# Block 1's rotary halves on VectorE, weight loads spread one per unit, weight rounding moved between units, and a separate load for the pooling columns

## The reference

```python
x = x + attn(cond(x))                                # cond: tanh scores, masked softmax, pooled
h = einsum("bsd,bdh->bsh", x, W[cat_ids]) + b[cat_ids]
tidx, tw = gate(h)                                   # 64 experts in 8 groups, 4 groups kept, top 8
y = sum over e of w_dense[:, e] * (silu(h @ wg[e]) * (h @ wu[e])) @ wd[e]
x = x + y + (silu(h @ ws_g) * (h @ ws_u)) @ ws_d     # one shared expert
```

## Time and profile before

| what | value |
|---|---|
| median of 3 runs | 741.04 us (739.32 to 742.67) |
| the profiled execution | 741.32 us |
| span of its trace | 739.5 us |
| TensorE busy | 709.9 us, 96% of the span |
| VectorE busy | 547.2 us, 74% |
| ScalarE busy | 444.7 us, 60% |
| GpSimd busy | 425.2 us, 57% |
| mean granted TensorE clock | 0.989 of full speed |

### The profile page before, as it was taken

How to read it: one execution, slowest core, us unless ns; L and a number is a source line. 1 busy time by engine, 2 the same in 40 slices (tenths; PEclk the granted TensorE clock), 3 DMA queues, 4 the chain that set the end, 5 groups by cost and what they waited for, 6 DMA issues and landing times.

```text
span 739.5 us, 15765 instructions
## 1 busy us (share of the span) xinstructions
PE 709.9 (96%) x5628; PEld 547.5 (74%) x5628; DVE 547.2 (74%) x1144; ACT 444.7 (60%) x857; POOL 425.2 (57%) x352
## 2 busy tenths in 40 slices
PE   8878899999999999999999999999999999999997
PEld 7756676677877778777787777777787777877885
DVE  5766659886598676887688865987768876886664
ACT  3865766568455765568555684557654685555553
POOL 2644488665466644556455654666455564666665
PEclk9998999999999999999999999999999999999999
DMA  8453542445433434434454463434535345444451
GB/s 279 143 199 90 148 108 82 130 106 157 103 123 111 140 110 116 143 96 143 109 120 132 108 154 104 121 108 137 119 115 140 100 142 117 101 123 147 129 134 44
DMA packets 66750, 93.00 MB, mean 126 GB/s; under 512 B 7760, under 2 KB 26640, under 8 KB 66672
## 3 DMA queue, kind: packets, MB, share of 16 engines
q1 hardware_dynamic: 62784, 88.07, 43.4%
q10 hardware_dynamic: 3888, 3.93, 1.5%
HBM read 88.37 MB, written 3.15 MB: 124 GB/s over the span
## 4 chain that ended last, share of the span: by engine, by line
PE 72%; DVE 11%; ACT 9%; issue 3%; POOL 2%; DMA 2%; SPq 1%; POOLq 0%; ACTq 0%; DVEq 0%
PE banks L979 70%; DVE act_w L946 3%; DVE hid L958 2%; ACT s_t L402 2%; ACT hid_hi L535 2%; POOL hid_lo L633 2%; ACT banks L523 1%; ACT L523 1%; ACT L402 1%; PE banks L1059 1%; SPq L269 1%; DMA k_rope<-rope_sum 1%; DVE head_max L704 1%; DVE s_t L703 1%; ACT v_blk L389 1%
## 5 line engine op out<-in xcount | busy, mean ns | idle before, releaser
L633 POOL TENSOR_TENSOR hid_lo<-hid,hid_hi 128x512 fp32r<-128x512 f32 (+1 forms) x264 | 341.9, 1295 | 275.4 <-ACT hid_hi L535 270.3
L946 DVE TENSOR_TENSOR act_w<-banks,cwb 128x512 f32<-128x512 f32 x254 | 174.6, 687 | 126.6 <-ACT banks L523 123.5
L523 ACT ACTIVATE banks<-banks 128x512 f32<-128x512 f32 x254 | 147.2, 582 | 141.3 <-PE banks L979 138.9
L535 ACT CAST hid_hi<-hid 128x512 fp32r<-128x512 f32 (+1 forms) x264 | 162.7, 616 | 76.8 <-DVE hid L958 75.1
L958 DVE TENSOR_TENSOR hid<-act_w,banks 128x512 f32<-128x512 f32 (+1 forms) x264 | 181.3, 687 | 24.8 <-PE banks L979 2.7
L979 PE MATMUL banks<-c_hi,wg_hi 128*128 128x512 f32 x264 | 119.2, 452 | 4.2 <-DVE act_w L946 4.2
L979 PE MATMUL banks<-hid_hi,wd_hi 128*128 128x512 f32 (+1 forms) x264 | 107.1, 406 | 4.7 <-POOL hid_lo L633 4.4
L979 PE MATMUL banks<-hid_hi,wd_lo 128*128 128x512 f32 (+1 forms) x264 | 104.0, 394 | 0.0
L979 PE MATMUL banks<-hid_lo,wd_hi 128*128 128x512 f32 (+1 forms) x264 | 104.0, 394 | 0.0
L979 PE MATMUL banks<-c_lo,wg_hi 128*128 128x512 f32 x264 | 103.9, 394 | 0.0
L979 PE MATMUL banks<-c_hi,wg_lo 128*128 128x512 f32 x264 | 103.9, 394 | 0.0
(11 more groups left out here) (158 smaller groups left out, 805.7 us busy)
## 6 DMA issues: line engine op xcount, KB each, us to landing
cwb<-cw_scratch SPq DMA_DIRECT2D x254, 256.0 KB, 3.7
k_blk<-in_cond_w SPq DMA_DIRECT2D x112, 64.0 KB
xf<-in_x_feat SPq DMA_DIRECT2D x8, 256.0 KB, 4.1
out_feat<-y ACTq DMA_DIRECT2D x8, 256.0 KB, 3.4
wg_raw<-in_we_gate SPq DMA_DIRECT2D x7, 256.0 KB, 5.5
wu_raw<-in_we_up SPq DMA_DIRECT2D x7, 256.0 KB, 5.8
wd_raw<-in_we_down SPq DMA_DIRECT2D x7, 256.0 KB, 5.9
xf<-in_x_tok SPq DMA_DIRECT2D x6, 256.0 KB, 2.8
```

What stands on the lines that cost most here:

```text
L523: nc.scalar.activation(dst, gate_bank(p)[:, :], ACT.Silu).then_inc(S["silu_done"], 1)
L535: nc.scalar.copy(hid_hi[0:n, p % NH, :], hid[0:n, p % NH, :]).then_inc(S["hi_ready"], 1)
L633: nc.gpsimd.tensor_sub(hid_lo[0:n, p % NH, :], hid[0:n, p % NH, :], hid_hi[0:n, p % NH, :].bitcast(F32)).then_inc(S["lo_ready"], 1)
L946: nc.vector.tensor_mul(act_w[:, p % NH, :], gate, weight)\
```

## The change

It has five parts. (1) Block 1's two rotary halves are added by VectorE (they were added by GpSimd) right after c_lo of block 0, and the key half is moved to k_rope by a VectorE copy (it was a DMA on SP's queue). Step 5 of block 1 on TensorE waits for the copy. (2) SP's quarter tiles 14 to 23 are no longer issued in one go: the units 2 to 11 of block 0 issue one each, behind the unit's cwb load, and unit 12 issues the shared expert's. (3) A table SPLITS says which unit of block 0 rounds which quarter tile: 4 takes 10; 6 to 16 take 11 to 21; 26, 27 and 28 take 22, 23 and 24. (4) The first 34 columns of w (w1, b1, vcol, which were at its end) come in a DMA of their own, first of all; the rest of w comes after the first x block with a semaphore of its own (proj_in), and the fold moves behind scores(0) on TensorE. On ScalarE pool_exp(0) moves ahead of the copies of the folded weights. (5) The seven x blocks are issued by ScalarE at its start, x tokens of block 1 by ScalarE too, block 0's residual load moves behind the condition matrices on SP, the blank matmuls go from 14 to 8, and pool_scores(2) moves from behind step 17 to behind step 16 of block 0 on TensorE.

```diff
@@ SP
-            sp.dma_start(c[:, :], consts).then_inc(S["consts_in"], 16)
-            sp.dma_start(w[:, :], weights).then_inc(S["consts_in"], 16)
+            cond = W_COLS["kvT"][0]
+            sp.dma_start(w[:, 0:cond], weights[:, 0:cond]).then_inc(S["cond_in"], 16)
+            sp.dma_start(c[:, :], consts).then_inc(S["consts_in"], 16)
+            sp.dma_start(pt_i, prompt).then_inc(S["prompt_in"], 16)
             sp.dma_start(xf_in[0], x_feat[:, bass.ts(0, TOK)]).then_inc(S["x_in0"], 16)
-            sp.dma_start(pt_i, prompt).then_inc(S["prompt_in"], 16)
+            sp.dma_start(w[:, cond:], weights[:, cond:]).then_inc(S["proj_in"], 16)
...
-            sp.wait_ge(S["c2tok_ps"], 1)
-            for i in range(14, NSPLIT):
-                weight_load(i)
-            sp.dma_start(wg_raw[:, NPAIR, :], ws_gu).then_inc(S["ws_in"], 16)
-            sp.dma_start(wd_raw[0:F, NPAIR, :], ws_down).then_inc(S["ws_in"], 16)
-            attention_loads("keys", 1)
...
+                if not prev and 2 <= p < 12:
+                    if p == 2:
+                        sp.wait_ge(S["c2tok_ps"], 1)
+                    weight_load(p + 12)
@@ ScalarE
-            act.wait_ge(S["consts_in"], 32)
+            for i in range(1, NBLK):
+                act.dma_start(xf_in[i], x_feat[:, bass.ts(i, TOK)]).then_inc(S["x_in1" if i < 4 else "x_in2"], 16)
+            act.wait_ge(S["cond_in"], 16)
+            act.wait_ge(S["consts_in"], 16)
             pool_hidden(0)
+            pool_exp(0)
+            act.wait_ge(S["proj_in"], 16)
@@ ScalarE and GpSimd, in the unit
+        SPLITS = {4: 10, **{p: p + 5 for p in range(6, 17)}, 26: 22, 27: 23, 28: 24}
-                if not prev and BEFORE_UNITS <= p + 1 <= NSPLIT:
-                    split(p + 1)
+                if not prev and p in SPLITS:
+                    split(SPLITS[p])
@@ GpSimd
-            rope_add(1)
@@ VectorE, after rotate(1) and rest_of_input(0, 0)
+                    dve.wait_ge(S["rot_ready"], 2)
+                    dve.wait_ge(S["rope_score_ps"], 1)
+                    nc.vector.tensor_add(rope_sum[:, :], rot[:, 0, :], rot[:, 1, :]).then_inc(S["rope_summed"], 1)
+                    keys_moved(1)
@@ TensorE
-        WARM_BLANK = 14
+        WARM_BLANK = 8
-                    if opening(blk):
-                        pe.wait_ge(S["krope_ready"], 1)
+                    if blk < 2:
+                        pe.wait_ge(S["krope_ready"], blk + 1)
```

More of the change, by code:

```diff
@@ L37 @@
 W_COLS, W_TOTAL = {}, 0
-for _n, _w in (("kvT", D), ("q", D), ("k", D), ("v", D), ("kr", 2 * ROPE), ("o", D), ("qr", 2 * ROPE),
-               ("w1", 32), ("b1", 1), ("vcol", 1), ("gate", E)):
+for _n, _w in (("w1", 32), ("b1", 1), ("vcol", 1), ("kvT", D), ("q", D), ("k", D), ("v", D), ("kr", 2 * ROPE), ("o", D),
+               ("qr", 2 * ROPE), ("gate", E)):
     W_COLS[_n] = (W_TOTAL, _w)
@@ L179, in adaln_attention_moe @@
         S = {}
-        for name in """consts_in prompt_in cats_in x_in0 x_in1 x_in2 xt_in0 xt_in1 xt_in blank pt_blank
+        for name in """cond_in consts_in proj_in prompt_in cats_in x_in0 x_in1 x_in2 xt_in0 xt_in1 xt_in blank pt_blank
                 vrep_ready onehot_ready pool_chain pool_spread
@@ L284, in attention_loads @@
                     sp.dma_start(xf[:, :], x_feat[:, bass.ds(blk * TOK, TOK)]).then_inc(S["res_in"], 16)
-                elif p == 7 and blk >= 2 or p == "keys":
+                elif p == 7 and blk >= 2:
                     sp.wait_ge(S["rope_summed"], blk + 1)
@@ L312, in _ @@
                 attention_loads(p, 0)
+            attention_loads(0, 0)
             for i in range(6, 14):
@@ L337, in unit_loads @@
                     sp.dma_start(cwb[:, p % NCW, :], src).then_inc(cwb_in[p % NCW], 16)
+                if not prev and 2 <= p < 12:
+                    if p == 2:
+                        sp.wait_ge(S["c2tok_ps"], 1)
+                    weight_load(p + 12)
+                elif not prev and p == 12:
+                    sp.dma_start(wg_raw[:, NPAIR, :], ws_gu).then_inc(S["ws_in"], 16)
+                    sp.dma_start(wd_raw[0:F, NPAIR, :], ws_down).then_inc(S["ws_in"], 16)
             pipeline(unit_loads)
@@ L668, in after_chain, with keys_moved @@
                 dve.wait_ge(S["dve_chain"], blk * CHAIN + steps[0])
+            def keys_moved(blk):
+                dve.wait_ge(S["rope_summed"], blk + 1)
+                nc.vector.tensor_copy(k_rope[:, :], rope_sum[ROPE:2 * ROPE, :]).then_inc(S["krope_ready"], 1)
             def attention_step(p, blk):
@@ L674, in attention_step @@
                     if p == 2 and opening(blk):
-                        dve.wait_ge(S["rope_summed"], 1)
-                        nc.vector.tensor_copy(k_rope[:, :], rope_sum[ROPE:2 * ROPE, :]).then_inc(S["krope_ready"], 1)
+                        keys_moved(0)
                     h = p - 1
@@ L886, in _ @@
             last.then_inc(S["vrep_ready"], 1)
+            dve.wait_ge(S["consts_in"], 16)
             dve.wait_ge(S["prompt_in"], 16)
@@ L1120, in _ @@
                 mm(U[1][:, 0:P], pool_pt[:, 0, :, :].rearrange("p s j -> p (s j)"), pool_pt[:, 0, :, :].rearrange("p s j -> p (s j)"))
-            pe.wait_ge(S["consts_in"], 32)
-            first, width = W_COLS["k"][0], 2 * D + 2 * ROPE
-            mm(A2[:, 0:width], W["kvT"], w[:, first:first + width]).then_inc(S["fold_ps"], 1)
             def warm(n, dst=U[1]):
@@ L1166, in pool_out @@
                 last.then_inc(S["pooled_ps"], 1)
+            pe.wait_ge(S["cond_in"], 16)
+            pe.wait_ge(S["consts_in"], 16)
             pool_hidden(0)
@@ L1171, in _ @@
             pool_scores(0)
+            pe.wait_ge(S["proj_in"], 16)
+            first, width = W_COLS["k"][0], 2 * D + 2 * ROPE
+            mm(A2[:, 0:width], W["kvT"], w[:, first:first + width]).then_inc(S["fold_ps"], 1)
             pool_hidden(1)
@@ L1183, in _ @@
                     pool_hidden(2)
-                elif p == 17:
+                elif p == 16:
                     pool_scores(2)
@@ L1312 @@
         "weights": np.concatenate([np.asarray(a) for a in (
+            L0_cond_W1, np.tile(np.asarray(L0_cond_b1), TILES)[:, None], np.tile(np.asarray(L0_cond_v), TILES)[:, None],
             np.asarray(L0_attn_W_kv_down).T, L0_attn_W_q, L0_attn_W_k_up, L0_attn_W_v_up, swapped(L0_attn_W_k_rope),
-            L0_attn_W_o, swapped(L0_attn_W_q_rope), L0_cond_W1, np.tile(np.asarray(L0_cond_b1), TILES)[:, None],
-            np.tile(np.asarray(L0_cond_v), TILES)[:, None], np.asarray(L0_ffn_gate_w).T)], 1),
+            L0_attn_W_o, swapped(L0_attn_W_q_rope), np.asarray(L0_ffn_gate_w).T)], 1),
         "consts": shape_constants(),
```

19 lines of the change are left out of this document (7 added, 12 removed).

## The result

The changed kernel takes 734.88 us (median of 7 runs, 734.17 to 738.99), the kernel before 741.04 (7 runs, 739.32 to 744.76): a ratio of 0.9933, 95% interval 0.9914 to 0.9953. The forecast was 733.2 with a range of 729.8 to 737.3. The profiled execution took 734.65 us, with a span of 732.8 against 739.5: 6.7 us less, where the sum of the terms said 7.8.

What follows compares the result with a forecast made beforehand. TensorE, busy 96% of the span, bounds the kernel, so only its idle and slow stretches can be won. Opening -1.0, k_rope wait -4.3, weight rests -2.9, small costs +0.3 and +0.1 sum to -7.8: 733.2 us, range 729.8 to 737.3.

Steps and rivals of the forecast that it cites:

- the clock: Low clock in block 0, half speed from 65.3 to 71.4 us: taken to stay, nothing counted for it.
- term 3: Opening, before unit 0: fewer blank matmuls and the 34 columns first win 1.0 us (0 to 2.5).
- term 1: Block 1's rotary step: TensorE's wait for k_rope goes, cw is late next; 4.3 us won (4.2 to 4.9).
- transposes to unit 9, with units 4 to 8: Block 0 up to unit 9: the new weight rest in unit 4 costs 0.3 us (0 to 1.6).
- term 2: Units 17 to 26 of block 0, freed of quarter tiles, win 4.0 us; net 2.9 after unit 28's stall.
- unit 27 to block 1: Unit 28's gate waits for quarter tile 22, now split in unit 26: a new stall of 1.1 us.
- The rival in which hid_lo alone holds VectorE up: Units 17 to 26: removing quarter tiles wins nothing, 736.1 us; in the 0.22 shared with opening and SP failures.
- this rival: Opening gets longer because w lands later: +1.0 in place of -1.0, 735.2 us; in a shared chance of 0.22.
- pool_out(0) at 12 to 13: Opening: start time in us of this TensorE operation, named as a sign that the forecast is right.
- the low clock goes too: Half-clock stretch before unit 9 shrinks: at most 3.0 us more, 730.2; 0.15 together with fewer stalls.
- SP late: Added issues make cwb late for VectorE in block 0: up to 2 us back, 735.2; in a shared 0.22.
- act_w waiting for cwb in units 5 to 12: VectorE in block 0: a wait named as a sign that the forecast is wrong; no size given.

Runs made afterwards that it cites:

- rotary: Kernel before with only the new rotary step (VectorE adds the halves and copies to k_rope): 735.65 us, ratio 0.9941.
- early: Changed kernel with the last three weight rests moved from units 26, 27, 28 to units 17, 18, 19: 737.78 us, ratio 0.9967.
- splits: Kernel before with only the new table of which unit rounds which quarter tile: 737.25 us, ratio 0.9960.
- x_on_sp: Changed kernel with the seven x loads issued by SyncE again instead of ScalarE: 735.30 us, ratio 0.9924.
- blank14: Changed kernel with 14 blank matmuls in place of 8: 735.57 us, ratio 0.9940.
- blank12: x_on_sp with 12 blank matmuls in place of 8: 734.82 us, ratio 0.9924.
- split25: old_front with the last three weight rests one unit earlier, in units 25, 26, 27: 733.50 us, ratio 0.9909.
- old_front: Changed kernel with the opening of the kernel before; rotary step, weight rests and loads one per unit stay: 735.39 us, ratio 0.9934.
- front: Kernel before with only the changed opening: 744.51 us, ratio 1.0051.
- old_front_early: Changed kernel with the opening of the kernel before and the last three weight rests in units 17 to 19: 735.23 us, ratio 0.9931.
- warm16: split25 with 16 warm matmuls in place of 9 ahead of the transposes of cw: 734.11 us, ratio 0.9915.

## Why the prediction was right, and where it was not

The total was in the range and it was faster, as forecast; one step had the wrong sign, and a gain that was not in the sum covered part of it. That the total missed by only 1.1 us (by span, 6.7 won for 7.8) is in part luck: the opening was wrong by 2.9, and the clock, which the forecast left alone, gave 1.9 of it back in this execution. Without that the run would still have been in the range, at about 736.5. In the second set of runs the same kernel had a median of 737.16, just inside the range's end. By profile, forecast and measured:

| step | forecast | measured |
|---|---|---|
| term 3, opening, to unit 0 | -1.0 | +1.90 |
| term 1, gate of unit 1 to the transposes of cw | -4.3 | -4.36 |
| transposes to unit 9, with units 4 to 8 | +0.3 | -1.56 |
| units 9 to 16 | 0 | 0.0 |
| term 2, units 17 to 26 | -4.0 | -3.89 |
| unit 27 to block 1 | +1.1 | +1.04 |
| the rest of the program (pool_scores +0.1) | +0.1 | +0.2 |
| sum | -7.8 | -6.7 |

**Term 1** was right in place, size and next limit. cw was ready 8.88 us after c_lo's end, where 8.5 to 9.2 had been allowed for; the rotary kernel gives the same 5.98 us with nothing else changed. The Trainium skill (GPSIMD Engine Reference, Key points) names, for the interfaces that GpSimd and VectorE share, VectorE instructions in a 2-port perf mode or with two SBUF inputs. The 1.32 us of L761 in the kernel early, for 0.22, is of the second kind, and the trace agrees. The copy that went from 0.42 to 0.83 has one input; no trace shows in which mode it ran.

**Term 2** was right, and splits shows it alone. The reason given, that VectorE is held up by GpSimd's quarter tiles, is now shown by early: three rests put back beside the routing cost 2.17 us in units 20 to 23. The rival in which hid_lo alone holds VectorE up is out, since with the rests gone the units run like block 2's (21.80 and 21.81 for 21.70). But the reason was too narrow: the second of the two delays in early ends with a hid_lo.

**Term 3 failed** (-1.0 forecast, +1.90 measured), at the step "from 0 (the loads are the limit) to 2.5 (TensorE is the limit); I take 1.0". A loss was kept for a rival, and this rival came, larger than it was priced (+1.0). Two things were missing. First, the sum followed only w: "the 34 columns no longer wait". But hidden(0) needs block 0 of x as well, issued fourth on SyncE, at 2.15 us, and ScalarE's seven loads are issued from 0.94 to 4.54 us, three of them ahead of it. It landed at 7.54 (2.15 + 5.39 in the chain); x_on_sp has it for 5.63. The large w took 6.7 us from issue to landing, twice the 3.4 of the earlier trace rows, as that rival had assumed. Second, 14 blank matmuls did more than fill time. At the start a blank takes 0.24 us (3.78 / 16), where a warm matmul of the same shape takes 0.126 later (2.27 / 18); the forecast's end of the blanks, 4.7, came at 5.11 for this reason. Behind 14 of them hidden(0) takes 0.43; after only 8 it takes 0.66 and the fold 1.44 instead of 0.81, and full rate is there only by 12.8. The hole of 2.57 us is not needed for this: x_on_sp, with one of 0.52, has the same 0.66 and 1.44. blank14 gives 1.45 us back by pool_out(0), x_on_sp 1.89, and both together (blank12) 2.45, so the two causes overlap. The Trainium skill, DMA: Bandwidth & Descriptors, Issuing engines are not separate DMA queues, spoke against this part; x_on_sp agrees with it (the 2.1 us). In the forecast it had weighed as a rival only. Of the signs that the forecast named, pool_out(0) at 12 to 13 missed (15.82).

**The clock** was left as it is, because the idle ahead of the stretch at 65.3, 2.53 us for head_max, was held to stay. It did not: it is 1.42 in the changed kernel:

```profile
63.50 1.15 PE L992 MATMUL banks<-k_blk,q_sb 32*32 32x128 f32 x64 [1.42 <-DVE head_max L712]
```

The half-clock stretch behind the wait for cw now falls into the pick matmuls (3.68 us in place of 1.99), and the later wait is shorter for it. All fourteen profiles divide by this. In six (the changed kernel twice, x_on_sp, early, split25, blank12) the pick matmuls ran slow, the wait was 1.4 to 1.5 us, and the 64 score matmuls behind it took 1.15. In the eight others the picks took 1.99, the wait was 2.5 to 4.2 us, and the 64 took 1.61 to 1.96, for a stretch of half clock began before or in them. The 1.56 us won up to unit 9 are therefore not safe: old_front and split25, alike up to there, stand on different sides. The second profile of the changed kernel has the short wait, but a stretch of 3.4 us right behind it, and needs 28.51 us from its transposes (53.30) to unit 9 (81.81), against 27.40 in the first and 28.96 before. The rival "the low clock goes too" thus held in one execution and in part in the other. (Its price of at most 3.0 us was worked out from a window of 6.10 us; the stretch itself is 6.8 us long, 64.9 to 71.7.)

**SP late** is a rival that I counted out too soon, and its sign, act_w waiting for cwb in units 5 to 12, came. "SP ran ahead of the use by several units" does not hold in the changed kernel. A row of VectorE's waits in the changed kernel, 60 to 115 us (us in total, times, longest; split25 has 5.2, 5, 1.6):

```profile
DVE act_w L959 <- DMA cwb<-cw_scratch: 4.6, 5, 1.9
```

Before has one such wait, of 1.0 us, in the same stretch. SyncE issues almost without a pause in units 8 to 11, 3.38 us for each unit (2.86 before): four of the next block's condition matrices (1.91; they go into k_blk's buffer), cwb (0.52) and the added weight load (0.59), with the rest in steps between them. From 76 to 90 us it waits for nothing there, where before it waits 2.9 us in all for act_w to free a cwb buffer. The added loads also share the DMA engines with cwb, which takes 4.6 us to land from 72 to 92 us (median) and 3.6 before; no run parts the two. split25 shows the issues, from SyncE's queue:

```profile
79.46 1.90 SPq L300 DMA_DIRECT2D k_blk<-in_cond_w  x4
81.48 0.52 SPq L332 DMA_DIRECT2D cwb<-cw_scratch  x1
82.05 0.59 SPq L270 DMA_DIRECT2D wu_raw<-in_we_up  x1
82.84 1.90 SPq L300 DMA_DIRECT2D k_blk<-in_cond_w  x4
```

In the first profile of the changed kernel TensorE hides the late cwb. In unit 12 it paid 0.81 us in the second, 0.56 in early, 1.29 in split25 and 1.89 in blank12. It paid nothing there in the kernels that keep the weight loads in one piece (before, rotary, splits, front), nor in six profiles with loads per unit; four of these six (old_front, old_front_early, blank14, warm16) had the long half-clock stretch ahead, which would give SyncE time (argued, not tested). Loads per unit were not tried alone, so their share of the total stays open, as does the best place for them.

**The scatter** stays open too. What decides, from one execution to the next, on which side a kernel falls was not found; it is worth up to 2.4 us at unit 9. So one profile can't rank kernels that lie 1 us apart, while it can show a place. Nor is it shown that split25 beats the changed kernel: its interval (0.9894 to 0.9924) overlaps the first of the changed kernel (0.9914 to 0.9953) and lies under the second (0.9931 to 0.9967). What is shown is the 1.0 us at unit 28, in one profile of each kernel.

## What to carry to other kernels

When a load is moved to a second issuing engine, list every small transfer that the first instruction on the path still needs and count the bytes now issued ahead of each; here the transfer that was not moved became late. A GpSimd instruction can cost most where nothing waits for it, when VectorE has a short instruction with both inputs in SBUF beside it: place such work where VectorE reads PSUM or stands, and look for the bill some units later. Before a gain in a profile is put down to the change, profile the same kernel twice; here the place of a stretch at half clock was worth up to 2.4 us, nearly as much as term 2.
